# Second feed-forward by seven block products instead of eight, its weight factors made beside attention

## The reference

```python
# layer 1 attention: 32 query heads, 8 key/value heads of 128, rotary angles on q and k, softmax(q k / sqrt(128)) v, @ wo
x = x + tanh(g_xattn[1]) * attention(norm(x), ctx, ctx, mask, wq, wk, wv, wo)
# layer 1 feed-forward: W1 = W_base + masked Fourier factors (ranks 32 and 8, three experts) times enc0, enc1
x = x + tanh(g_ffn[1]) * (norm(x) @ W1.T + b_base)
```

## Time and profile before

| | us |
|---|---|
| median of 3 runs | 3052.45 (3050.22 to 3052.49) |
| the profiled execution | 3052.67 |
| its span, first to last instruction | 3050.9 |

### The profile page before, as it was taken

The page is one execution under the profiler, slowest core; times in us unless marked ns, Lnnn a source line. Parts: engine busy times, 40 slices in busy tenths (PEclk is TensorE's granted clock), DMA queues, the critical chain, the costliest instruction groups (busy, mean ns, idle before and its releaser), DMA issues.

```text
span 3050.9 us, 40952 instructions
## 1 busy us (share of the span) xinstructions
PE 2985.9 (98%) x14752; PEld 2504.4 (82%) x14752; DVE 1976.0 (65%) x4642; ACT 1253.2 (41%) x2626; POOL 1271.5 (42%) x1028
## 2 busy tenths in 40 slices
PE   9999999999999999999999899999999999999999
PEld 7888778887777878877888788888888888888887
DVE  4432478887665686678667867666766676666432
ACT  4111366675333322232224455554454444454210
POOL 2422388885322577768776343311111111111231
PEclk9999999999999999999999999999999999999999
DMA  7332421113555654455444776765566556575321
GB/s 247 127 123 98 168 57 63 70 56 112 165 193 195 196 163 111 111 155 159 111 111 127 226 232 230 237 219 169 182 206 202 181 174 220 175 272 168 137 92 56
DMA packets 317461, 479.91 MB, mean 157 GB/s; under 512 B 26108, under 2 KB 155516, under 8 KB 315468
## 3 DMA queue, kind: packets, MB, share of 16 engines
q1 hardware_dynamic: 316540, 475.84, 48.9%
q10 hardware_dynamic: 720, 1.44, 0.1%
HBM read 319.92 MB, written 157.29 MB: 156 GB/s over the span
## 4 chain that ended last, share of the span: by engine, by line
PE 58%; DVE 4%; DMA 1%; ACT 1%; POOL 1%; issue 0%; SPq 0%; ACTq 0%; DVEq 0%; POOLq 0%
PE PB L150 18%; PE PB L151 18%; PE PB L152 18%; PE PB L2382 3%; DMA at_wol<-wod 1%; DVE qp_r L2178 0%; PE PB L2681 0%; DVE at_ptl L2521 0%; ACT at_ss L2429 0%; DVE at_ss L2501 0%; POOL qp_a L2208 0%; DVE qp_r L2186 0%; DMA qp_in<-xod 0%; DVE PB L2181 0%; DVE qp_r L2179 0%
## 5 line engine op out<-in xcount | busy, mean ns | idle before, releaser
L2544 POOL TENSOR_TENSOR at_ql<-at_qf,at_qh 128x512 fp32r<-128x512 f32 x128 | 166.3, 1300 | 914.1 <-ACT at_qh L2422 914.1
L2429 ACT ACTIVATE at_ss<-at_ss,at_sm,at_bs 128x256 f32<-128x256 f32 x512 | 302.0, 591 | 336.6 <-DVE at_sm L2505 336.6
L150 PE MATMUL PB<-at_woh,at_ah 128*128 128x512 f32 x1024 | 401.6, 392 | 5.4 <-POOL at_wol L2551 3.5
L151 PE MATMUL PB<-at_wol,at_ah 128*128 128x512 f32 x1024 | 400.6, 391 | 0.0
L152 PE MATMUL PB<-at_woh,at_al 128*128 128x512 f32 x1024 | 399.5, 390 | 0.0
L2535 DVE SCALAR_TENSOR_TENSOR at_xt<-PB,gt,at_xt 128x512 f32<-128x512 f32 x256 | 191.9, 750 | 258.0 <-PE PB L152 258.0
L150 PE MATMUL PB<-qp_b,qp_a 128*128 128x512 f32 x896 | 350.1, 391 | 8.0 <-POOL qp_a L2208 2.6
L151 PE MATMUL PB<-qp_b,qp_a 128*128 128x512 f32 x896 | 348.7, 389 | 0.0
L152 PE MATMUL PB<-qp_b,qp_a 128*128 128x512 f32 x896 | 348.7, 389 | 0.0
L2208 POOL TENSOR_TENSOR qp_a<-qp_raw,qp_a 128x512 fp32r<-128x512 f32 x192 | 257.8, 1354 | 104.9 <-ACT qp_a L2103 102.2
L2441 ACT ACTIVATE at_pth<-PB 128x512 fp32r<-128x512 f32 x256 | 139.1, 596 | 240.7 <-PE PB L2382 240.7
(11 more groups left out here) (290 smaller groups left out, 7464.2 us busy)
## 6 DMA issues: line engine op xcount, KB each, us to landing
at_woh<-wod SPq DMA_DIRECT2D x48, 1024.0 KB, 6.3
at_wol<-wod SPq DMA_DIRECT2D x48, 1024.0 KB, 8.8
qp_raw<-in_wq SPq DMA_DIRECT2D x32, 1024.0 KB, 5.4
qd<-qp_r SPq DMA_DIRECT2D x256, 128.0 KB, 2.5
at_qf<-qd SPq DMA_DIRECT2D x128, 256.0 KB, 3.5
at_rawo<-in_wo SPq DMA_DIRECT2D x32, 512.0 KB, 5.0
wod<-at_woh SPq DMA_DIRECT2D x16, 1024.0 KB, 5.5
wod<-at_wol SPq DMA_DIRECT2D x16, 1024.0 KB, 6.2
```

Source lines behind the costliest of these rows:

```text
L150: pe.matmul(o, ah, bh, start=start, stop=False)
L151: pe.matmul(o, ah, bl, start=False, stop=False)
L2429: m = act.activation(at_ss[s][:, c, :], at_ss[s][:, c, :], ACT.Exp, bias=z[:, 4 + c:5 + c], scale=at_bs[:, qn % 2, 8 + 2 * b + c % 2:9 + 2 ...
L2544: self.pool.tensor_tensor(at_ql[n % 3][:, :], at_qf[n % 2][:, :], asf(at_qh[n % 3][:, :]), ALU.subtract).then_inc(*inc("at_pool", ("q", n)))
```

## The change

1. The first feed-forward no longer splits W1: `w1d` is one fp32 array, and the buffers are four.
2. During attention periods 40 to 72 (`WF = 40`), one step of `wf_schedule` behind each period builds the seven factors of W1's 2 x 2 blocks, a quarter q of the rows at a time: GpSimd sums, ScalarE high parts, GpSimd low parts. Factors 0 to 2 stay in SBUF. Factors 3 to 6 go through a ring of one slot, `f1_ring`, and SyncE stores them to `w1f`; they are loaded again at attention's end.
3. The second feed-forward works on pairs of tiles: seven products of 4 x 3 matmuls, results added up by VectorE. The factors of the normalized tiles are built by VectorE (sums), ScalarE (high) and VectorE or GpSimd (low).
4. The last four query turns come behind every second attention period.

```diff
@@ first feed-forward, pieces (ACT and DVE)
-                    act.activation(f0_keep[s][0], f0_wr[s], ACT.Copy).then_inc(*inc("f0_act", ("keep", c)))
...
-                    on.wait_ge(*at("f0_act", ("keep", c)))
-                    dve.tensor_tensor(f0_keep[s][1], w_, asf(f0_keep[s][0]), ALU.subtract).then_inc(*inc("f0_dve", ("keep", c)))
@@ qp_schedule
             for tn in range(2):
                 for pair in Q_BLOCKS[-1]:
+                    yield
                     do.turn(pair, tn)
                     yield
@@ at_schedule
-                if u < 10 or u in (NU - 1, NU, NU + 1):
+                if u < 14 or WF <= u < WF + 33 or u > NU - 2:
                     yield
@@ new: factors of the weight
+        def wf_schedule(do):
+            for q in range(4):
+                do.fetch(q)
+                yield
+                for i in range(7):
+                    do.make(q, i)
+                    yield
+            do.last()
+            yield
+            # WfScalar
+            def make(self, q, i):
...
+                if i > 3:
+                    on.wait_ge(*at("f1_ws", (q, i - 1)))
+                elif i == 3 and q:
+                    on.wait_ge(*at("f1_ws", (q - 1, 6)))
+                self.act.activation(f1_part(q, i, 0), f1_factor(i), ACT.Copy).then_inc(*inc("wf_act", ("w", q, i)))
+            # WfGpsimd
+            def make(self, q, i):
...
+                if i == 0:
...
+                    pool.tensor_tensor(f1_s1[:, :], a21, a22, ALU.add).then_inc(*inc("wf_pool", ("s", q, 3)))
...
+                    pool.tensor_tensor(a21, a11, a21, ALU.subtract).then_inc(*inc("wf_pool", ("s", q, 2)))
...
+                pool.tensor_tensor(f1_part(q, i, 1), f1_factor(i), asf(f1_part(q, i, 0)), ALU.subtract).then_inc(*inc("wf_pool", ("w", q, i)))
...
+            # WfSync
+            def store(self, q, i):
+                on = self.on
+                on.wait_ge(*at("wf_act", ("w", q, i)))
+                on.wait_ge(*at("wf_pool", ("w", q, i)))
+                self.sp.dma_start(w1f[i][:, :, q, :], asf(f1_ring[:, :, :])).then_inc(*landed("f1_ws", (q, i)))
...
+            def make(self, q, i):
+                if i > 3:
+                    self.store(q, i - 1)
@@ f1_tensor
+            def product(p, i):
...
+                claim(4 + (7 * p + i) % 4, ("f1_act", ("sum", p, 0)) if i == 0 else ("f1_dve", ("sum" if i < 3 else "f", p, i)))
+                for c in range(4):
+                    m = three(pe, f1_bank(p, i), (x[:, 0, c, :], x[:, 1, c, :]), (f1_w[i][0][:, c, :], f1_w[i][1][:, c, :]), c == 0, c == 3)
...
+            for p in range(F1_PAIRS):
+                for i in range(7):
+                    product(p, i)
+                    if i in (2, 3) and p + 1 < F1_PAIRS:
+                        flip(2 * p + i)
@@ f1_scalar: rows(2), rows(3), the scaled bias, then for each pair
+                first(p)
+                    factor(p + 1, 0)
+                    copy(p + 1)
+                    for i in (3, 1, 2, 4, 6, 5):
+                        factor(p + 1, i)
@@ f1_vector
+            for p in range(F1_PAIRS):
+                for i in range(1, 4):
+                    leave(p, i)
+                if p + 1 < F1_PAIRS:
+                    rest(p + 1, 0)
+                    sums(p + 1, (3, 1, 2, 5))
+                    rest(p + 1, 4)
+                    rest(p + 1, 6)
+                if p + 2 < F1_PAIRS:
+                    stats(2 * p + 4)
+                    stats(2 * p + 5)
+                for i in range(4, 7):
+                    leave(p, i)
@@ f1_sync: loads of the stored factors, in attention's tail
+            on.wait_ge(*at("at_pe", ("out", NG - 2, 7)))
+            load_w(4, 0)
+            load_w(4, 1)
```

More of the change, by code:

```diff
@@ L2230, in fetch_w @@
                 if pair < 2:
-                    on.wait_ge(*at("f0_w1s0", ("low", C - 2)))
-                    on.wait_ge(*at("f0_w1s1", ("low", C - 1)))
+                    for c in range(4, C):
+                        on.wait_ge(*at(f"f0_w1s{c % 4}", c))
                 else:
@@ new lines, in copy, with first @@
+            def copy(p):
+                on.wait_ge(*at("f1_pe", ("T", 2 * p + 1, 0)))
+                if p:
+                    on.wait_ge(*at("f1_dve", ("t", p - 1, 2)))
+                act.activation(f1_b12[:, :, :], f1_turned(2 * p + 1, 0), ACT.Copy).then_inc(*inc("f1_act", ("b12", p)))
+            def first(p):
+                on.wait_ge(*at("f1_pe", ("M", p, 0)))
+                if p:
+                    on.wait_ge(*at("f1_dve", ("sum", p - 1, 4)))
+                else:
+                    on.wait_ge(*at("at_pe", ("values", NU - 1)))
+                act.activation(f1_c11[:, :], f1_bank(p, 0), ACT.Copy).then_inc(*inc("f1_act", ("sum", p, 0)))
@@ L2737, in f1_scalar @@
+            for _ in range(2):
                 yield
@@ L2775, in leave, with rest @@
[L2775 to L2783 removed]
+            def rest(p, i):
+                x, t, hf = f1_x[f1_slot(p, i)], 2 * p + (i == 6), int(i != 0)
+                on.wait_ge(*at("f1_act", ("x", p, i)))
+                dve.tensor_tensor(x[:, 1, :, :], f1_turned(t, hf), asf(x[:, 0, :, :]), ALU.subtract).then_inc(*inc("f1_dve", ("x", p, i)))
@@ new lines, in sums @@
+            def sums(p, which):
+                even, odd = ([f1_turned(2 * p + n, hf) for hf in range(2)] for n in range(2))
+                t1, t2, t3, t4 = (f1_t[f1_slot(p, i)][:, :, :] for i in (3, 1, 2, 5))
+                for i, o, a, b, done in ((3, t1, f1_b12[:, :, :], even[0], None), (1, t2, odd[1], t1, 3), (2, t3, odd[1], f1_b12[:, :, :], None),
+                                           (5, t4, even[1], t2, 1)):
+                    if i in which:
+                        f1_slot_free(on, p, i)
+                        on.wait_ge(*at("f1_pe", ("T", 2 * p + 1, 1)))
+                        on.wait_ge(*at("f1_act", ("b12", p)))
+                        if done is not None:
+                            on.wait_ge(*at("f1_dve", ("t", p, done)))
+                        dve.tensor_tensor(o, a, b, ALU.subtract).then_inc(*inc("f1_dve", ("t", p, i)))
@@ L2870, in f1_sync @@
             yield
-            on.wait_ge(*at("at_pe", ("out", NG - 1, 7)))
+            yield
+            load(3)
+            on.wait_ge(*at("at_xout3", NQ - 1))
             sp.dma_start(f1_bg[:, :], b1.partition_broadcast(P)).then_inc(*landed("f1_b", 0))
@@ L2911, in weave @@
                 next(att)
-            next(att)
-            next(f1)
-            for _ in range(4):
+            for _ in wf:
+                next(att)
+            for _ in range(7):
+                next(att)
                 next(f1)
-                next(att, None)
             for _ in att:
                 pass
-            next(f1)
+            for _ in f1:
+                pass
         def tensor(pe):
```

373 lines of the change are left out of this document (237 added, 136 removed).

## The result

The changed kernel takes 3078.22 us (median of 6, 3072.25 to 3080.92), the kernel before 3052.47 (6 runs): ratio 1.0079, 95% interval 1.0069 to 1.0090. It is slower, as forecast, but by 25.7 us and not by 9.6; it lies 3 us above the range of 3026 to 3075. The profiled execution took 3078.03 us, its span is 3076.2.

What follows compares the result with a forecast made beforehand. TensorE, busy 98% of the span, was taken as the bound: its instruction stream plus its waits. Terms -14.8 - 8.5 - 3.3 - 4.6 + 40.9 = +9.7 on 3052.7 gave 3062 us, range 3026 to 3075.

Steps and rivals of the forecast that it cites:

- the sign that was to refute it: Factors' stretch of attention: the forecast is wrong if the stretch 2012 to 2310 of before isn't at least 16 us longer.
- Part 5: Factors beside attention: ScalarE's wait for the one-slot ring's store closes a loop through SyncE, 13.1 us for 9.14; +40.9 us.
- the landing: Ring factor's store of 512 KB beside attention: lands after 4.2 us, taken from one earlier store right behind `at_qf`.
- my own formula: Factors beside attention: four quarters, three late loops each less 2.9 us hidden, plus 2 for an output tile, 3.4 for clock.
- the upper bound: Factors beside attention: loss of 55 us if the store lands after 5.5 us, the queue being fuller.
- the clock: TensorE on recovery behind each quarter's waits: clock falls after one of two waits, 4 x 1.7 / 2 = +3.4 us.
- Part 1: Second feed-forward: seven products for eight, -21.7 us for 96 fewer matmuls, +6.2 waits, +0.7 last add; -14.8 us.
- Part 2: First feed-forward: without the second weight's high/low split, two `f0hl` waits of 3.4 us and 1.7 of clock go; -8.5 us.
- Part 3: Attention's four query turns, moved behind every second period: 15.7 us lost becomes 12.4, a gain of 3.3.
- Part 4: Tail of attention: -2.7 us from waits at normalization and transposes, -1.9 from the flood of weight loads; together -4.6.
- the wait costs nothing: Rival, factors beside attention: ScalarE's idle time hides the store's landing; 3021 us (3015 to 3030), chance 0.14.
- Slower still: Rival: same loop on a fuller queue, plus VectorE bounding the second feed-forward; 3074 us (3068 to 3085), chance 0.18.

Runs made afterwards that it cites:

- store_alone: The changed kernel, but SyncE waits until each factor's store has landed before it issues anything else: 3065.99 us, ratio 1.0043.
- the three kernels of experiment 3: The early-store kernel with one or two ring-factor stores per quarter sent a slot late, 3033.14 and 3050.55 us, and the changed kernel with three, 3078.22 us.
- -10.9 alone: The kernel before without the high/low split of the second weight in the first feed-forward, the full weight stored instead: 3041.42 us, ratio 0.9967.
- early-store kernel: The changed kernel with each ring factor's store issued in the slot that makes it, ahead of the next fetch_q: 3018.84 us, ratio 0.9886.
- one-wait kernel: The early-store kernel with the first ring factor's store of each quarter one slot late, behind fetch_q: 3033.14 us, ratio 0.9936.

## Why the forecast was wrong, step by step

*Which way, and why slower:* right. The place (twelve periods), the chain (ScalarE's wait, `at_pth`, `at_ptl`, `values`, the next `fetch_q`, the store) came as said, and the sign that was to refute it didn't: the stretch that had to be at least 16 us longer is 61 longer.

*Part 5, the landing:* part 5 is the step that failed, its mechanism right and two of its terms too small; the landing is the first. I took 4.2 us from the earlier trace rows as "same size, same predecessor, same stretch" and didn't look at what is behind: that store has one of its own kind behind it and loads only after 4.2 us, this one 1 to 2 MB of loads from 0.6 us on. I had the right number for another queue, as `store_alone` shows, and one store of 16 that landed in 2.6 to 8.4 us in the same trace. With 5.3 my own formula gives 4 x (3 x 5.1 - 2.9) + 2 + 3.4 = 55.0 us for 40.9: 14 of the missing 20.4 us. Read from the starts of `at_pth`, the rows make it 65.0 us late for the 49.2 of the forecast (4 x 11.8 + 2): 15.8. The landing was in the forecast as the upper bound, whose 55 us are not its own sum, though: at 5.5 us the formula gives 51.2 without the 2 and the 3.4, and 56.6 with them. SyncE's wait for an output tile in the last quarter, for which I had 2 us, was there with 1.5.

*Part 5, the clock:* the second term. Behind the last wait of each row I priced 0.85 us, 3.4 in all; the stretches there lose 7.7: 4.3 more. With the 15.8 of the lateness and 0.6 in the mask's period that makes 20.7 for the missing 20.4, if 2.9 us a row are hidden, as I had it and as the three kernels of experiment 3 bear out. The trace of before had only single waits of 3.4 us, one with and one without a loss; I carried their mean over to rows of three.

*Part 1:* -16.9 for -14.8. The wait at the first pair was there (1.79 us, forecast 2.3), the 0.5 us in each later pair weren't, and the extra addition at the end cost its 0.7.
```profile
2929.16 0.47 PE L150 MATMUL PB<-f1w,f1x 128*128 128x512 f32 x1 [1.79 <-DVE f1xt L2963]
```
*Part 2:* -10.9 alone, for -8.5. Both waits and the clock as forecast; I had missed two waits for `f0xn` of 0.76 and 0.75 us behind the stalls, which went with them.

*Part 3:* -3.4 to -3.7 for -3.3. *Part 4:* the flood -2.2 for -1.9; the tail gave 0.9 for 2.7, the period of the last transposes being 1.0 us longer and a wait of 0.71 for `at_ptl` left.

*The rivals:* "the wait costs nothing" was 3021 us if the store went out ahead of `fetch_q`. That kernel, built, takes 3018.8: the sum of all other parts was right to 2 us, in part by luck, since by the table they come to -35.9 for -31.2, with errors of both signs (-3.7, -2.1, +1.8). "Slower still" had the right mechanism in its first half, the fuller queue, and a wrong second half, VectorE as the bound; its 3068 to 3085 us held the result.

## What to carry to other kernels

A store whose landing somebody waits for is priced with what is issued behind it too, and if the waiting engine also carries the work from which the next store's issue follows, the landing is paid in full in every turn of the loop; send the store out before the fetch that depends on that work, or give the buffer a second slot. Price TensorE's clock at the end of a row of waits apart from the waits. Before work is moved beside other work, look up which GpSimd operation stands in that place: a VectorE operation with two SBUF operands takes its length or gives it its own.

## What was not expected

- Three operations per slot cost more than six: 0.69 us becomes 2.6 beside a GpSimd subtraction of 2.3, and four weighings 4.46 for 1.14. Where VectorE was already in a run of such operations, GpSimd's took 3.26 for 1.29.
- The start of attention scatters by 4 us between two executions of the early-store kernel (period 1 at 14.6 and at 18.6 us ahead of the kernel before). That is as much as the smaller terms of this forecast; the stretch from period 42 to 71 doesn't have it: 0.64 and 0.63 us over the kernel before.
- TensorE's clock did not fall behind every wait, nor by the wait's length. In the changed kernel a wait of 2.19 us was followed by 5 us at a granted clock of 1.00, waits of 2.20 and 3.52 us by 5 us at 0.66; in the one-wait kernel one of 3.14 us was followed by 10 us at 1.00. What decides it was not settled.
